# Two mixture-of-experts FFNs in one kernel: units of the shared experts first, the routing in pieces between units, last products two units behind

## What is computed

```python
def ffn0(x):                                   # 2304 tokens x 256, layer-normed
    scores = sigmoid(x @ router_weight.T)      # 8 experts
    choice = scores + correction_bias
    group_scores = top_k(choice.reshape(-1, 2, 4), 2)[0].sum(-1)
    masked = where(in_best_group, choice, 0.0)
    topk_idx = top_k(masked, 2)[1]
    w = take(scores, topk_idx); w = w / (w.sum(-1) + 1e-20)
    comb = (one_hot(topk_idx, 8) * w).sum(1)
    y = einsum('tei,eih->teh', silu(x @ w_gate) * (x @ w_up), w_down)
    return einsum('teh,te->th', y, comb) + silu(x @ sw_gate) * (x @ sw_up) @ sw_down

def ffn1(x):
    scores = sigmoid(x @ gate_w.T + lb_bias)
    topw, topi = top_k(scores, 2); topw = topw / (topw.sum(-1) + 1e-8)
    for e in range(8):
        m = topi == e
        wmean = (topw * m).sum() / max(m.sum(), 1)
        out += where(m.any(-1), mlp_e(x) * wmean, 0)
    return out + shared_mlp(x)
```

## Time and profile before

| | |
|---|---|
| median of 3 runs | 814.58 us (813.88 to 816.41) |
| profiled execution | 820.07 us, its span 818.2 us |
| PE busy | 745.6 us, 91% |
| DVE, ACT, POOL busy | 583.7, 338.8, 127.3 us |
| prep of FFN 0, FFN 0 | about 131.7 to 150.7, to 327.6 us |
| prep of FFN 1, FFN 1 | about 602.9 to 617.6, to 815.3 us |
| mean granted clock of PE | 0.981 of 2.4 GHz |

### The profile page before, as it was taken

The page is one execution under the profiler, slowest core; times in us unless marked ns, Lnnn a source line. Parts: engine busy times, 40 slices in busy tenths (PEclk is TensorE's granted clock), DMA queues, the critical chain, the costliest instruction groups (busy, mean ns, idle before and its releaser), DMA issues.

```text
span 818.2 us, 13681 instructions
## 1 busy us (share of the span) xinstructions
PE 745.6 (91%) x4993; PEld 610.5 (75%) x4993; DVE 583.7 (71%) x1229; ACT 338.8 (41%) x595; POOL 127.3 (16%) x121
## 2 busy tenths in 40 slices
PE   3279996799999999999999999999998999999997
PEld 3259994699999999865444444444766999999997
DVE  6986767677777777847666666667786677777776
ACT  1214554433333333214777767665433333333332
POOL 0205651000000000070121542222500000000000
PEclk9999996999999999989999999999999999999999
DMA  8500000000000000082345664212200000000000
GB/s 322 208 1 1 0 2 0 1 1 1 1 2 2 0 0 0 2 194 70 81 102 77 118 112 98 41 20 78 127 0 1 1 20 21 1 21 19 2 20 20
DMA packets 21186, 36.54 MB, mean 45 GB/s; under 512 B 6301, under 2 KB 16957, under 8 KB 20489
## 3 DMA queue, kind: packets, MB, share of 16 engines
q1 hardware_dynamic: 16328, 33.12, 15.2%
q10 hardware_dynamic: 4800, 2.66, 2.0%
HBM read 25.79 MB, written 9.95 MB: 44 GB/s over the span
## 4 chain that ended last, share of the span: by engine, by line
PE 83%; DVE 11%; issue 2%; ACT 2%; DMA 2%; POOL 0%; SPq 0%; DVEq 0%; POOLq 0%
PE PS L1248 17%; PE PS L1250 17%; PE PS L1249 17%; PE PS L1507 7%; PE PS L1482 5%; PE PS L1491 5%; PE PS L1515 3%; PE PS L1256 2%; PE PS L1598 2%; DVE MX L1160 2%; PE PS L1331 1%; PE PS L1365 1%; PE PS L1276 1%; DMA x_in<-in_x 1%; PE PS L1565 1%
## 5 line engine op out<-in xcount | busy, mean ns | idle before, releaser
L1160 DVE TENSOR_REDUCE MX<-PS 128x2 f32<-128x576 f32 x144 | 108.7, 756 | 61.8 <-PE PS L1491 61.4
L1086 DVE SCALAR_TENSOR_TENSOR h<-PS,cmb,h 128x256 f32<-128x256 f32 (+1 forms) x342 | 143.9, 476 | 0.2 <-PE PS L1250 0.2
L692 ACT ACTIVATE PR<-PS 96x768 f32<-96x768 f32 x144 | 115.9, 807 | 55.7 <-PE PS L1482 55.2
L633 ACT ACTIVATE sg<-PS 128x384 f32<-128x384 f32 x114 | 56.1, 493 | 164.4 <-PE PS L1250 164.4
L1071 DVE TENSOR_TENSOR al<-aa,ah 128x384 fp32r<-128x384 f32 x114 | 63.6, 558 | 67.1 <-ACT ah L637 67.1
L637 ACT ACTIVATE ah<-aa 128x384 fp32r<-128x384 f32 x114 | 60.0, 526 | 84.0 <-DVE aa L1065 84.0
L1065 DVE TENSOR_TENSOR aa<-sg,PS 128x384 f32<-128x384 f32 x114 | 63.2, 554 | 25.7 <-ACT sg L633 25.2
L1248 PE MATMUL PS<-xTh,W1h 128*128 128x384 f32 x240 | 81.1, 338 | 0.0
L1249 PE MATMUL PS<-xTh,W1l 128*128 128x384 f32 x240 | 80.9, 337 | 0.0
L1250 PE MATMUL PS<-xTl,W1h 128*128 128x384 f32 x240 | 80.8, 337 | 0.0
L1248 PE MATMUL PS<-xTh,W0h 128*128 (+1 forms) x216 | 72.9, 338 | 0.0
(11 more groups left out here) (239 smaller groups left out, 1581.1 us busy)
## 6 DMA issues: line engine op xcount, KB each, us to landing
QS<-scrH SPq DMA_DIRECT2D x28, 144.0 KB, 4.3
W1raw<-in_w SPq DMA_DIRECT2D x1, 3840.0 KB, 12.2
W0raw<-in_w SPq DMA_DIRECT2D x1, 3456.0 KB, 11.3
scrH<-qh SPq DMA_DIRECT2D x8, 432.0 KB, 2.5
scrL<-ql SPq DMA_DIRECT2D x8, 432.0 KB, 2.9
wD<-in_wD SPq DMA_DIRECT2D x1, 2304.0 KB, 11.7
out_tokens<-h SPq DMA_DIRECT2D x6, 384.0 KB, 2.3
x_in<-in_x SPq DMA_DIRECT2D x2, 1024.0 KB, 6.2
```

What stands on the lines that cost most here:

```text
L692: A_(PR[0:KT, ca:cb + 1:cb - ca, :], PS[0:KT, b:b + 2, 0:CW], ACT.Exp).then_inc(s["e_exp"], 1)
L1086: ins = V.scalar_tensor_tensor(out=hj, in0=PS[:, b + t // 2, (t % 2) * D:(t % 2) * D + D], scalar=cmb[:, ds(g * GT + t, 1), e:e + 1].squee ...
L1160: V.tensor_reduce(MX[:, hf, z:z + NSH // 2 + 1:NSH // 2], PS[:, b:b + 2, 0:POS], AX_X, ALU.max).then_inc(s["e_mx"], 1)
```

## The change

Seven things, in both layers:

1. The units of the shared experts come first: units 0 to 5 (layer 0) or 0 to 11 (layer 1), group by group; then the 8 routed experts of group 0, of group 1 and so on.
2. `down` and `accumulate` are two units behind `gate_up` (`LAG`), and DVE's order in a unit is `aa` of n, accumulation of n - 2, `al` of n.
3. The routing is cut up, a piece after `al` of each of the first units: choice of groups (0), comparisons of experts 0 to 3 (1) and 4 to 7 (2), count (3), choice of two (4), weights (5), in layer 1 totals (6).
4. The small product of the sums goes into unit 9's `gate_up` (`SUM_N`), into free columns of that unit's bank, and `average` stands before `aa` of unit 9.
5. ACT does a sigmoid of one column (`unit`) after `lgT` of group 2 in the prep, which loads the table there.
6. `router_back` of group 5 stands in the middle of `gate_up(0)`; `down(1)`, whose output shares the bank, waits for the scores to be read.
7. A loop body is 8 units: in PE and DVE one group is written out and five are passes of the loop; on ACT all six are.

```diff
@@ SP
-            sp.wait_ge(s["f1_acc"], 10 * (g + 1))
+            sp.wait_ge(s["f1_acc"], NE * (g + 1) + NSHARED[1])
@@ ACT, prep of layer 0 (and of layer 1 in the same way)
                 if L is not None and g:
                     logits(L, g - 1, (g - 1) % 2, 6)
+                if L is not None and g == 3:
+                    A_(unit[:, :], unit[:, :], ACT.Sigmoid)
@@ DVE
-        def experts(L, gu, before_last=None):
+        def experts(L, before_last=None):
+            ns, units = NSHARED[L], NSHARED[L] + NG * NE
...
+            for n in range(ns):
+                if L == 1 and n == SUM_N:
+                    dve.wait_ge(s["f1_gu"], n + 1)
+                    average(n % 2)
+                gated(n, n % 2)
+                if n >= LAG:
+                    accumulate(n - LAG, (n - LAG) % NG, NE + (n - LAG) // NG, n % 2)
+                low(n, n % 2)
+                if n == 0:
+                    choose_groups(L)
+                if n == 1:
+                    compare(L, 0, NE // 2)
+                if n == 2:
+                    compare(L, NE // 2, NE // 2)
+                if n == 3:
+                    count()
+                if n == 4:
+                    chosen(L)
+                if n == 5:
+                    weigh(L)
+                if L == 1 and n == 6:
+                    totals()
+
             def body(r, first=False):
-                for k in range(per):
-                    n = r * per + k
-                    if first and k == 0:
-                        compare(L)
-                    gated(n, k)
-                    if first and k == 1 and L == 1:
-                        average()
-                    low(n, k)
-                    if first and k == 0:
-                        weigh(L)
...
+                for k in range(NE):
+                    n = r * NE + (ns + k)
+                    gated(n, k % 2)
+                    if first and k < LAG:
+                        accumulate(n - LAG, (n - LAG) % NG, NE + L, k % 2)
+                    else:
+                        accumulate(n - LAG, r + (k - LAG) // NE, (k - LAG) % NE, k % 2)
+                    low(n, k % 2)
...
             body(0, True)
-            with dve.Fori(1, NG // gu) as r:
+            with dve.Fori(1, NG) as r:
                 body(r)
+            accumulate(units - 2, NG - 1, NE - 2, 0)
             if before_last is not None:
                 before_last()
-            accumulate(NG * ne - 1, NG - 1, ne - 1, per - 1)
+            accumulate(units - 1, NG - 1, NE - 1, 1)
@@ PE
                 split3(PS[:, b, 0:GW], [(Gh[:, e, c], Gl[:, e, c], *xs[c]) for c in range(KC)])
+                if isinstance(n, int) and n == 0:
+                    router_back(L, NG - 1, 1, 7)
+                if L == 1 and isinstance(n, int) and n == SUM_N:
+                    pe.wait_ge(s["f1_tot"], 1)
+                    M(PS[:, 2 + b, GW:GW + 2 * NE], ones[:, :], tot[:, :], start=True, stop=True)
                 split3(PS[:, 2 + b, 0:GW], [(Uh[:, e, c], Ul[:, e, c], *xs[c]) for c in range(KC)]).then_inc(s[f"f{L}_gu"], 1)
...
+                if isinstance(n, int) and n == 1:
+                    pe.wait_ge(s[("f0_sig", "f1_lraw")[L]], 1)
...
+            for n in range(ns):
+                gate_up(n, n % NG, NE + n // NG, n % 2)
+                if n >= LAG:
+                    down(n - LAG, NE + (n - LAG) // NG, n % 2)
+
             def body(r, first=False):
-                for k in range(per):
-                    n = r * per + k
-                    gate_up(n, r * gu + k // ne, k % ne, k)
...
+                for k in range(NE):
+                    n = r * NE + (ns + k)
+                    gate_up(n, r, k, k % 2)
+                    down(n - LAG, NE + L if first and k < LAG else (k - LAG) % NE, k % 2)
```

More of the change, by code:

```diff
@@ L623, in sigmoid, with experts, unit @@
                 A_(sc[:, :, :], sc[:, :, :], ACT.Sigmoid).then_inc(s["f1_sig"], 1)
[L625 to L641, removed]
+        def experts(L):
+            def unit(n, b):
+                act.wait_ge(s[f"f{L}_gu"], n + 1)
+                A_(sg[:, b], PS[:, b, 0:GW], ACT.Silu).then_inc(s[f"f{L}_silu"], 1)
+                act.wait_ge(s[f"f{L}_mul"], n + 1)
+                wait(act, s[f"f{L}_dn"], n - 1)
+                A_(ah[:, b], aa[:, b], ACT.Copy).then_inc(s[f"f{L}_ah"], 1)
+            for n in range(NSHARED[L]):
+                unit(n, n % 2)
+            with act.Fori(0, NG) as r:
+                for k in range(NE):
+                    unit(r * NE + (NSHARED[L] + k), k % 2)
         act.wait_ge(s["d_a1"], 16)
@@ L748, in _ @@
                 logits(1, g - 1, (g - 1) % 2, 6)
+            if g == 3:
+                A_(unit[:, :], unit[:, :], ACT.Sigmoid)
         sigmoid(1, 7)
-        experts(1, 3)
+        experts(1)
     @block.vector
@@ L1005, in compare @@
                 own.settle()
-                key = sv
             else:
                 dve.wait_ge(s["f1_sig"], 1)
-                key = sc
-            for e in range(NE):
+        def compare(L, a, n):
+            key = (sv, sc)[L]
+            for e in range(a, a + n):
                 if e:
@@ L1037, in weigh, with totals @@
             own(V.tensor_tensor(sv[:, :, :], t3[:, :, :], rcp, ALU.mult))
+        def totals():
             own.settle()
@@ new lines, in body @@
+            def body(r, first=False):
+                for k in range(NE):
[6 more added lines that the diff above has]
+                    low(n, k % 2)
+                    if L == 0 and not first and LAG <= k < LAG + GT:
+                        tile_stats(r * NE + ns, r - 1, k - LAG)
@@ L1437, in down @@
                 ins.then_inc(s[f"f{L}_dn"], 1)
+            for n in range(ns):
+                gate_up(n, n % NG, NE + n // NG, n % 2)
+                if n >= LAG:
+                    down(n - LAG, NE + (n - LAG) // NG, n % 2)
             def body(r, first=False):
-                for k in range(per):
-                    n = r * per + k
-                    gate_up(n, r * gu + k // ne, k % ne, k)
-                    if L == 1 and first and k == 2:
-                        pe.wait_ge(s["f1_tot"], 1)
-                        M(PS[:, 7, 0:2 * NE], ones[:, :], tot[:, :], start=True, stop=True).then_inc(s["f1_sum"], 1)
-                    if not first or k >= 1:
-                        down(n - 1, (k - 1) % ne, (k - 1) % per)
+                for k in range(NE):
+                    n = r * NE + (ns + k)
+                    gate_up(n, r, k, k % 2)
+                    down(n - LAG, NE + L if first and k < LAG else (k - LAG) % NE, k % 2)
             body(0, True)
-            with pe.Fori(1, NG // gu) as r:
+            with pe.Fori(1, NG) as r:
                 body(r)
-            down(NG * ne - 1, ne - 1, per - 1)
+            down(units - 2, NE - 2, 0)
+            down(units - 1, NE - 1, 1)
         pe.wait_ge(s["rw_split0"], 2)
@@ L1636 @@
 S_LEAD = -2
+SUM_N = 9
 NLATE = 2
```

62 lines of the change are left out of this document (25 added, 37 removed).

## The result

The median of 20 runs is 817.58 us (804.97 to 921.35), beside 815.79 us (813.88 to 831.90, 20 runs) for the kernel before on the same chip. The predicted 805.2 us is what the best of the 20 runs took (804.97), and the range of 802.0 to 808.7 holds two of them. The ratio to the kernel before is 0.9941, with a 95% interval of 0.9914 to 0.9967: 0.6% faster, where 1.2% was forecast. This ratio leaves out executions over 1.5% above the fastest of their kernel, ten of the 20 here, and so it is smaller than the medians say; in this case the spread itself is the subject.

The account below looks back on a forecast made before the run. PE was taken to bound the kernel at 3.147 us a unit, with savings only where it stands still at the FFN ends. -4.4 and -5.0 us made -9.4 us off the 814.58 us median: 805.2 us, range 802.0 to 808.7.

Parts of the forecast that it names:

- The terms of the FFNs: Summed savings and costs at the starts, ends and preps of both FFNs: -4.4 us for FFN 0, -5.0 us for FFN 1.
- the fall at the start of FFN 1: Behind FFN 1's starting pauses the clock was 0.72 over 6.00 us; removing this was to save 1.7 us.
- my terms for FFN 0: FFN 0: start pause -3.5, slow clock -1.7, front -0.26, end wait -0.45, prep load +0.7, `aa` waits +0.84; sum -4.4 us.
- For FFN 1: FFN 1: pauses -1.2 and -2.35, clock -1.7, front -0.26, end -0.45, prep +0.9, `aa` wait +0.1; sum -5.0 us.
- The waits for `aa`: Early units of FFN 0: PE waits 0.57 us at unit 3 and 0.27 us at unit 6; bounds 0 and 2.35 us.
- The waits for `al` at the ends: End of each FFN: a wait of 0.95 us in place of 1.4, saving 0.45 us each.
- The moved load: Sigmoid table load on ACT in each prep: +0.7 us in layer 0, +0.9 us in layer 1, bounds 0 and 1.5.
- Part 3: Rest of the program: nothing else changes; seven more jumps back cost 0, at most 0.7 us.
- Rival 1: Preps: pauses from the moved load drop the clock, 1.7 us a fall, giving 806.9 or 808.6 us; chance 0.14.
- Rivals 2 to 5: Prep hides load (802.8 us, 0.13); load doubles (807.8, 0.04); jumps slow it (0.04); order fails (808.7, within 0.05).

Follow-up runs that it names:

- dense_start: Changed kernel with 3 filler products in place of 1 or 2 in the first eight units of the attention's first turn; median 809.18 us.
- the shifted one: Changed kernel with 28 filler products between the prep and FFN 0; 811.13 to 820.67 us (6 runs) and 810.56 to 830.22 us (13 runs).
- warm12_no_load: Changed kernel with 12 filler products, not 8, ahead of the first row of scores, and without the moved table load; median 806.55 us (4 runs).
- warm12: Changed kernel with 12 and not 8 filler products ahead of the first row of scores; median 808.34 us.
- l0_only: Changed kernel with FFN 1 as in the kernel before and only the table load of layer 0 moved; median 818.53 us.
- before_warm12: Kernel before with 12 and not 8 filler products ahead of the first row of scores; median 817.75 us.
- warm10_no_load: Changed kernel with 10 filler products, not 8, ahead of the first row of scores, and without the moved table load; median 807.63 us.
- filled: warm10_no_load with filler products added in three PE pauses ahead of the first prep; median 804.20 us, ratio 0.9887 to the kernel before.

## Why the prediction was wrong

- **The terms of the FFNs held, and that the whole came to 9.4 us is partly luck.** With the attention calm in both kernels the difference is 9.4 us by medians and 8.5 by the fastest runs. In the pair of profiles the two FFNs and the stretch with the prep of FFN 1 give 8.1 us; the fall at the start of FFN 1, 1.7 us of my sum, was missing there, and an earlier start of FFN 0, 1.2 us that I did not have, stood in its place. From first to last product my terms for FFN 0 give -3.5 - 1.7 - 0.45 + 0.84, and +0.38 for the transposes moved inside: -4.4 us; measured -4.7. For FFN 1 they give -1.2 - 2.35 - 1.7 - 0.45 + 0.1 + 0.38 = -5.2; measured -5.3 where the clock had fallen before, and -3.7 where it had not.
- **The waits for `aa`** were one of 0.2 us in place of 0.57 and 0.27: DVE's pieces fitted better than I had added up. The waits for `al` at the ends, two of 0.87 us, were put at 0.95.
- **The moved load** cost 0.52 and 0.82 us in the preps, where I had 0.7 and 0.9. The 0.7 was also a slip: router 4 at 146.48 + 0.88 and `lgT` 1.8 us later give 149.16 and not 149.3, so +0.55. What I missed is that its cover was there without moving it: I took the load of the earlier trace rows for a cost at the FFN's start and never asked whether ACT would stand idle at that place once the transposes had moved into unit 0. No rival was that the change is faster without one of its parts.
- **The step that failed** is Part 3: "Nothing else of the program changes", and with it "the waits named are fixed lengths, so I take the same 9.4 us off it". A wait ahead of thin work is not worth a fixed time: in the profiled executions its price was 2.6 us before and 13.7 us after, so the 9.4 us became 0.6 us of span (-2.0 ahead of FFN 0, -4.7, +11.1, -5.3, and +0.3 in the two stretches between). That fall of the clock stands in the trace of before at 360 us. The page's row of slices isn't near full speed all along, as I wrote ahead of the prediction: it has an 8 among the nines at 348 to 368 us, and a 6 at 123 to 143 us, for the falls ahead of FFN 0. I read only the windows at the FFNs. The fall at 360 us lasted 7 us and cost 2.6 us in that execution (221.72 less 219.11), 13.7 us in the profile of the changed kernel (232.82 less 219.14) and 17.3 in the next (236.43).
- **Rival 1** had the right mechanism, a pause that drops the clock, at the wrong place: it looked at the pauses that the change makes, of 0.38 to 0.77 us, behind which no profile shows a fall, and priced a fall at 1.7 us, as long as one in the midst of full work. Behind the wait for `KS` the work is thin, and a fall lasted from 7 to 51 us. Not one of the rivals was that a stage nobody touches gets slower.
- **The spread** was in sight as well: the profiled execution lay 5.5 us above the median of the three runs. I carried it along as an offset that stays, when it was the sign of a time that differs between executions of one kernel. The three runs of before, 813.88 to 816.41, showed little of a spread that reached 834.5 us in 124.
- Rivals 2 to 5 did not come: the load took 1.28 us where it was moved to, the jumps back cost nothing (FFN 1 is as long as the sum says), and the order did what it says.

## What to carry to other kernels

Ahead of a prediction list every fall of the granted clock in the trace of before, not only those that the change touches, and write beside each what pause starts it and how dense the work behind it is: a fall ahead of full products lasted 3.4 us and cost 1.7, one ahead of thin products lasted up to 51 us and cost up to 17, and differently in each execution. A wait of a microsecond ahead of thin work is worth filling; the filler of 12 lengthened its stretch by 1.5 us and brought eight of nine runs within 2.7 us of each other, where the changed kernel spread over 16 us and more. And where two parts of a change stand next to each other, ask what each still brings once the other is in.

## What the runs showed of the hardware

- The wait for `KS` differs between executions of one kernel: 1.06, 1.43 and 1.72 us in the three profiles of the changed one. In the kernels with 8 filler products (`dense_start` aside, where its own filler covered most of it) it was 0.71 to 1.72 us, and only behind the 0.71 did the clock stay. How long it then stayed at 0.50 doesn't follow the pause: 17 us (in two pieces) behind 0.84, 7 us behind 0.88, 41 behind 1.02, 41 behind 1.06, 10 behind 1.26, 44 behind 1.29, 17 (in two pieces) behind 1.43, 51 behind 1.72. Without a fall the attention took 219.0 to 219.2 us in six kernels, one of them the shifted one with its pause of 0.71 us.
- The filler does not cover every pause of this stage. In `warm12_no_load` the clock fell to 0.50 for 3.4 us from 469 us on, behind a wait of 0.85 us for the row maxima `MX`, and the attention took 220.29 us; `warm12` has the same wait, 0.84 us, and no fall.
- In the slow stretch PE was busy for 39.89 of 40.00 us and the clock still did not come back.
- Pauses of 1.0 and 1.7 us at the start of FFN 1 lowered the clock in the profile of before and in that of `l0_only`, and the same ones in `before_warm12` did not.
- What stays open: why a few runs of the filled kernels are some 6 to 9 us above the rest (`warm12` one of nine, `before_warm12` two of 12, `warm10_no_load` two of 12, `filled` one of six), with a mean clock of 0.973 to 0.983. No profile fell on one of them. With 10 filler products a wait for `KS` longer than the filler would do it: two more products cover 1.24 us, and 1.72 has been seen. With 12 it would not by these numbers, since four more cover 2.5 us. A fall behind the wait for `MX` is another candidate. Both are argued, not shown.
